# A memory-attention block between two expert layers: the second layer's hidden units in their own rows only, copied to the other rows by SBUF transfers, and a new order on GpSimd and VectorE

## The reference, cut to what matters

```python
for c0 in range(0, S, CHUNK):                      # 8 chunks of 128 tokens
    g = _grad_fn(W_state, k[:, sl], v[:, sl]) * GRAD_SCALE
    gn = jnp.maximum(jnp.linalg.norm(g, axis=-1, keepdims=True), EPS)
    g = g * jnp.minimum(MAX_GRAD_NORM / gn, 1.0)
    (S_state, W_state), Wtraj = jax.lax.scan(step, (S_state, W_state), xs)
    h = jax.nn.silu(jnp.einsum('btd,btod->bto', q[:, sl], W1t))
    outs.append(jnp.einsum('bto,btpo->btp', h, W2t))
...
out = out * jax.lax.rsqrt(jnp.mean(out * out, -1, keepdims=True) + EPS) * norm_g
```

## Time and profile before

| | |
|---|---|
| median of 3 runs (lowest, highest) | 765.0 us (764.88, 766.89) |
| span of the profiled execution | 767.1 us |
| mean granted TensorE clock in it | 0.961 |
| TensorE matmul / weight load busy | 88% / 76% |
| VectorE, ScalarE, GpSimd busy | 79%, 57%, 31% |

### The profile page before, as it was taken

The page is one execution under the profiler, slowest core; times in us unless marked ns, Lnnn a source line. Parts: engine busy times, 40 slices in busy tenths (PEclk is TensorE's granted clock), DMA queues, the critical chain, the costliest instruction groups (busy, mean ns, idle before and its releaser), DMA issues. The chain is left out here.

```text
span 767.1 us, 15489 instructions
## 1 busy us (share of the span) xinstructions
PE 673.5 (88%) x5715; PEld 580.6 (76%) x5715; DVE 606.4 (79%) x1373; ACT 438.1 (57%) x1105; POOL 240.0 (31%) x201
## 2 busy tenths in 40 slices
PE   5719999999597889999999999999998469999996
PEld 2218899898476777988879888887976257989985
DVE  0677788773488999999999999999985869887851
ACT  1325575662367667677666877767463446557550
POOL 0023453123311416052350714416061053722202
PEclk9958999999899999999999999999999769999999
DMA  9949637170411004013040311302103715834301
GB/s 343 411 176 349 221 117 254 36 214 22 126 54 56 1 1 141 27 56 112 21 146 1 105 63 56 112 1 77 35 12 100 274 49 166 281 100 163 130 15 35
DMA packets 58226, 89.26 MB, mean 116 GB/s; under 512 B 6960, under 2 KB 49072, under 8 KB 58032
## 3 DMA queue, kind: packets, MB, share of 16 engines
q1 hardware_dynamic: 46176, 70.28, 26.5%
q0 software_dynamic: 3840, 10.49, 4.2%
q10 hardware_dynamic: 8144, 7.61, 3.2%
HBM read 74.73 MB, written 22.02 MB: 126 GB/s over the span
## 5 line engine op out<-in xcount | busy, mean ns | idle before, releaser
L721 PE MATMUL ps<-moe_normedT_high,weights_high_up 128*128 128x320 f32 x252 | 80.8, 321 | 0.4 <-DVE moe_hidden_low L539 0.2
L722 PE MATMUL ps<-moe_normedT_low,weights_high_up 128*128 128x320 f32 x252 | 78.1, 310 | 0.0
L723 PE MATMUL ps<-moe_normedT_high,weights_low_up 128*128 128x320 f32 x252 | 78.1, 310 | 0.0
L1233 POOL TENSOR_TENSOR att_o_rs<-att_o_mean,minus_half 128x4 f32<-128x4 f32 x16 | 16.2, 1013 | 194.7 <-DVE att_o_mean L1491 194.7
L721 PE MATMUL ps<-weights_high_down,moe_hidden_high 128*128 128x256 f32 x256 | 73.3, 286 | 1.0 <-DVE weights_rows L547 1.0
L539 DVE SCALAR_TENSOR_TENSOR moe_hidden_low<-ps,moe_hidden_high 128x256 fp32r<-128x256 f32 x128 | 53.9, 421 | 24.3 <-ACT moe_hidden_high L676 20.2
L723 PE MATMUL ps<-weights_high_down,moe_hidden_low 128*128 128x256 f32 x256 | 71.4, 279 | 0.0
L722 PE MATMUL ps<-weights_low_down,moe_hidden_high 128*128 128x256 f32 x256 | 71.3, 279 | 0.0
L635 ACT CAST weights_high_down<-weights_raw_down 128x256 fp32r<-128x256 f32 x96 | 35.1, 407 | 38.9 <-PE ps L723 32.7
L721 PEld LDWEIGHTS ps<-weights_high_down,moe_hidden_high 128*128 128x128 f32 x256 | 48.1, 188 | 4.3 <-issue 4.3
L315 DVE TENSOR_TENSOR weights_low_down<-weights_raw_down,weights_high_down 128x256 fp32r<-128x256 f32 x128 | 49.8, 415 | 0.0
(11 more groups left out here) (328 smaller groups left out, 2073.6 us busy)
## 6 DMA issues: line engine op xcount, KB each, us to landing
weights_raw_up<-in_w SPq DMA_DIRECT2D x16, 1024.0 KB, 9.3
weights_raw_down<-in_w SPq DMA_DIRECT2D x16, 1024.0 KB, 8.3
first_xt<-in_xT SPq DMA_DIRECT2D x8, 1024.0 KB, 7.7
weights_rows<-x SPq DMA_DIRECT2D x8, 1024.0 KB, 5.6
out_x<-weights_rows SPq DMA_DIRECT2D x8, 1024.0 KB, 4.5
weights_rows<-x ACTq DMA_DIRECT2D x7, 1024.0 KB, 5.6
weights_rows<-x SPq DMA_DIRECT2D x2, 512.0 KB, 4.2
weights_raw_up<-in_w_x SPq DMA_DIRECT2D x1, 768.0 KB
```

Of the source, the lines that this page charges most:

```text
L721: mm(dst, high_l, high_r, start=start, stop=False)
L722: mm(dst, high_l, low_r, start=False, stop=False)
L723: return mm(dst, low_l, high_r, start=False, stop=stop)
L1233: g.tensor_tensor(o_rs[:, n], o_mean[:, n], t["minus_half"][:, n], ALU.pow).then_inc(o_rs_ready, 1)
```

## The change

`second_hidden` on TensorE puts the four sequences of each side only into that side's own rows: half as many products, and the result is four columns blocks wide instead of eight. ScalarE does two Silus of 64 rows x 512 columns in place of one of 128 x 1024. SyncE then copies each half to the other rows, from SBUF to SBUF, as two transfers of 64 rows x 2 KB (`double_hidden`), and `decayed_hidden` on VectorE now also waits for both of them. `second_scores` on TensorE needs own rows alone and does not wait for them.

GpSimd's `query_decay` and `mix` of the next chunk stand ahead of the first output power, and `hidden` stands between the second output power and the second residual sum of the step before. VectorE has softplus ahead of the output mean, theta ahead of the small products, and five of the eight `bn_stats` ahead of the gradients, three behind them. `last_step` has the same new order, but its hidden units are made as before, in both halves.

```diff
+            def double_hidden(c):
+                sp.wait_ge(hid2_ready, c + 1)
+                for n, own, other in SIDES:
+                    sp.dma_start(hid2[other, n, :], hid2[own, n, :]).then_inc(hid2_doubled, 16)
+            double_hidden(0)
+                if c + 2 < NCH:
+                    double_hidden(c + 1)
...
@@ -1244,18 +1254,19 @@
                 if first:
                     query_decay(c, True)
                     mix(c, True)
-                elif not last:
-                    hidden(c, par, False)
                 if norm_too:
                     norm(c + 2)
-                output_power(c, 0)
                 if not last:
                     query_decay(c + 1, False)
                     mix(c + 1, False)
+                output_power(c, 0)
+                if not last:
                     residual(c, par, 0)
                 output_power(c, 1)
                 if last:
                     return
+                if c + 2 < NCH:
+                    hidden(c + 1, 1 - par, False)
                 residual(c, par, 1)
             setup()
...
@@ -1478,6 +1501,7 @@
             def decayed_hidden(c):
                 dve.wait_ge(hid2_ready, c + 1)
+                dve.wait_ge(hid2_doubled, 32 * (c + 1))
                 v.tensor_tensor(hid2_ab[:], hid2[:], AB[:], ALU.mult).then_inc(hid2_ab_ready, 1)
             def second_scores(c, par):
...
@@ -1552,19 +1577,27 @@
             def step(c, par, first, norm_too=True):
                 split_turned(c + 1)
-                if not first:
+                if first:
+                    norm_sums(c)
+                    norm_products(c, par)
+                    softplus(c, par)
+                    thetas(c, par)
+                    gradients(c, par)
+                else:
                     slope_of(c)
+                    softplus(c, par)
                     output_mean(c - 1, 1)
                     residual(c)
-                    softplus(c, par)
                     gated_output(c - 1, 1 - par, 1)
-                gradient_norms(c, par)
-                if first:
-                    softplus(c, par)
-                elif norm_too:
-                    stats_of(c + 2)
-                thetas(c, par)
-                gradients(c, par)
+                    norm_sums(c)
+                    thetas(c, par)
+                    norm_products(c, par)
+                    if norm_too:
+                        batch_stats(c + 2, range(0, EARLY_STATS))
+                    gradients(c, par)
+                    if norm_too:
+                        batch_stats(c + 2, range(EARLY_STATS, B))
+                        aggregate(c + 2, range(B))
                 if first:
                     carry_scans(c, True)
                     decay_scans(c, True)
...
@@ -1758,7 +1791,9 @@
             def second_hidden(c):
                 act.wait_ge(pre2_made, c + 1)
-                s.activation(hid2[:], wide(DD), ACT.Silu).then_inc(hid2_ready, 1)
+                for n, own, _ in SIDES:
+                    last = s.activation(hid2[own, n, :], wide(DD)[own, 0:HALF, :], ACT.Silu)
+                last.then_inc(hid2_ready, 1)
             def retrieve(c):
                 act.wait_ge(ret_made, c + 1)
...
@@ -2034,11 +2069,13 @@
                 pe.wait_ge(qab_ready, c + 1)
                 if not first:
                     pe.wait_ge(x2_turned_copied, 2 * c)
-                for b in range(B):
-                    for rows in (slice(0, D), slice(D, P)):
-                        mm(wide(DD)[rows, b, :], state[par][:, b, D:2 * D], QAB[:, b, :], start=True, stop=False)
-                    for rows in (slice(0, D), slice(D, P)):
-                        last = mm(wide(DD)[rows, b, :], grad_w1[:, b, :], P1[:, b, :], start=False, stop=True)
+                for i in range(HALF):
+                    for n, own, _ in SIDES:
+                        b = n.start + i
+                        mm(wide(DD)[own, i, :], state[par][:, b, D:2 * D], QAB[:, b, :], start=True, stop=False)
+                    for n, own, _ in SIDES:
+                        b = n.start + i
+                        last = mm(wide(DD)[own, i, :], grad_w1[:, b, :], P1[:, b, :], start=False, stop=True)
                 last.then_inc(pre2_made, 1)
             def last_second_hidden(c, par, h):
```

More of the change, by code:

```diff
@@ L1044, in memory_attention @@
     HW = HALF * CH
+    EARLY_STATS = 5
     w_high, w_low, w_o, mean, x_norm, x_res = (
@@ L1116, in memory_attention @@
     pre2_made, hid2_ready, hid2_ab_ready = (sem(n) for n in ("pre2_made", "hid2_ready", "hid2_ab_ready"))
+    hid2_doubled = sem("hid2_doubled")
     hh_made, p2_ready, ret_made, ret_copied = (sem(n) for n in ("hh_made", "p2_ready", "ret_made", "ret_copied"))
@@ L1289, in moments_of, with batch_stats, aggregate @@
                     v.bn_stats(stats[:, b, :], x_norm[:, b, :]).then_inc(stats_done, 1)
+                aggregate(c, batches)
+            def batch_stats(c, batches):
+                if batches.start == 0:
+                    dve.wait_ge(x_loaded, 16 * c + 16)
+                    dve.wait_ge(x_normed, B * c - HALF)
+                for b in batches:
+                    v.bn_stats(stats[:, b, :], x_norm[:, b, :]).then_inc(stats_done, 1)
+            def aggregate(c, batches):
                 dve.wait_ge(stats_done, B * c + batches.stop)
@@ L1454, in residual, with norm_sums, norm_products @@
                 v.scalar_tensor_tensor(dpre[:], wide(C)[:, :, D:P], 0.5, slope[:], ALU.mult, ALU.mult).then_inc(dpre_ready, 1)
-            def gradient_norms(c, par):
+            def norm_sums(c):
                 dve.wait_ge(squared, 3 * c + 3)
                 v.tensor_reduce(nsum[:], squares[:], AX.X, ALU.add).then_inc(nsum_ready, 1)
+            def norm_products(c, par):
                 dve.wait_ge(nsum_ready, c + 1)
```

## The result

The changed kernel is slower. Its median is 778.38 us (777.24 to 781.35, four runs) against 764.94 us of the kernel before on the same chip (763.22 to 766.89, four runs): a ratio of 1.0172, 95% interval 1.0141 to 1.0204. The forecast was 767.3 us with a range of 761.5 to 772.0, so the time lies above the whole range. The profiled execution took 777.97 us at a span of 775.8.

The account below looks back on a forecast made before the run. TensorE's own work was taken to set the 46.17 us step; afterwards a loop through the transfers, 46.26 + 0.25 = 46.5 us. Seven chunks at +0.33 gave +2.3 on the 765.0 us median: 767.3 us, range 761.5 to 772.0.

Parts of the forecast that it names:

- its loop: Chain from one `decayed_hidden` to the next over VectorE, TensorE, ScalarE and the transfers: 46.26 us, 46.5 with the copies.
- the transfers' size: From the Silus' end to both transfers landed: 2.45 us taken, bounds 1.9 and 3.2; with hand-overs 2.54.
- the zero for the ends: Gains and losses in steps 0 and 6 set against each other: 0, with 2 us to either side.
- the clock: Listed only as a sign of being wrong: granted clock under 1.00 where TensorE now waits longer; no size.
- the copies' 0.25: VectorE's copies of end values, held by GpSimd's work, and what follows them: +0.25 us a step.
- TensorE -1.8 us: `second_hidden` on TensorE keeps 16 of 32 products: 1.8 us less a step.
- the Silus 1.18: ScalarE's two Silus of 64x512 in place of one of 1.03 us: 1.17 us, +0.14.
- the gradients earlier by some 3 us: VectorE's new order brings the gradients some 3 us earlier; nothing waits for that.
- the slope 0.68: VectorE's L1447, no longer held by GpSimd's first residual sum: 0.69 us instead of 1.81, -1.12.
- idle time before `decayed_hidden`: VectorE arrives there about 0.6 us before the second transfer lands and is idle, in every steady step.
- 7 x 0.33: Seven chunks have the transfers, each with a loop 0.33 us longer than 46.17: +2.3 us.
- costs all it may: Rival: transfers of 3.0 us, or copies and `mix` taking turns; steps of 47.1 to 47.4 us, 771 to 773; chance 0.19.

Follow-up runs that it names:

- ends_on_scalar: The changed kernel with the four copies of end values on ScalarE, not VectorE: 779.69 us, 1.0174 of the kernel before.
- ends_scalar_filled: ends_on_scalar with eight products on TensorE that nobody reads, ahead of `retrieve`: 770.43 us, 1.0079 of the kernel before.
- eager: The changed kernel with the first transfer started behind the first Silu, not behind both: 773.46 us, 1.0101 of the kernel before.
- filled: The changed kernel with eight 128x512 products on TensorE that nobody reads, ahead of `retrieve`: 775.33 us, 1.0125 of the kernel before.
- transfer_only: The kernel before with the second layer in own rows and the two transfers, old orders of GpSimd and VectorE: 771.28 us, 1.0076 of the kernel before.
- pool_as_before: The changed kernel with GpSimd's order of before, transfers and VectorE's order as changed: 779.78 us, 1.0181 of the kernel before.

## Why the prediction was wrong, by its own steps

The mechanism was the one it named, and its loop closes on the new trace; three terms of the sum failed: the transfers' size, the zero for the ends, and the clock, which it had left out. From `decayed_hidden` at 359.58: to `turn_keys` 16.65 us (forecast 16.54), from there to the rates 21.57 (21.28, and the copies' 0.25 on top), to the keep rates 2.01 (2.02), to the Silus' end 3.88 (3.88), to the next `decayed_hidden` 2.93 (2.54): 47.04 against 46.51.

- *Right:* TensorE -1.8 us; the Silus 1.18; the gradients earlier by some 3 us (36.56 us behind `decayed_hidden`, was 39.68), and without gain; the slope 0.68; idle time before `decayed_hidden` (1.1 us, forecast 0.6); 0.25 us for the copies, shown by ends_on_scalar and ends_scalar_filled, although all of 1.4 us is lost on VectorE.
- *Transfers, the mis-sized term.* The "2.45" from the Silus' end to both landed measured 2.84 (2.81 from the first issue), and the whole hop 2.93, not 2.54: a transfer takes 2.18 to 2.30 us, not 2.05, and the second issue comes 0.51 us behind the first, not 0.4. That is 0.39 of the 0.53 us by which the step missed its forecast. Taking the 64 KB load's 1.9 us as the base was too low; the middle of its bounds (1.9 to 3.2) was closer. eager shows that each tenth of it lengthens the step by about a tenth.
- *"0 with 2 us to either side" for the ends, wrong.* There is a loss at every chunk. Without falls (filled) `decayed_hidden` of chunk 0 comes 1.0 us later after the first gates, the five steps lose 1.0, 0.9, 0.9, 0.9 and 1.3 us, the last 1.4, because it had been short for want of statistics and now has the full loop (47.04, was 45.69), and the rest 0.4. That makes 7.8 us, where 7 x 0.33 had been forecast. The prediction had named the last one, but had set it off against gains in steps 0 and 6. In step 6 the held factor did fall from 1.86 to 0.17 us (L1495), but VectorE's wait ahead of it grew from 0.97 to 1.76 us, and the loop shows nothing of it. The first step is shorter in transfer_only (46.26 us, was 46.86), but not in filled (47.87).
- *The clock, left out of the sum.* It stood only under what would make the forecast wrong. I estimate the cost of the changed kernel's falls at 3 to 5 us: 1.0172 against 1.0125 for filled is 0.5%, with intervals that overlap, and in the profiles attention, from its first gate addition to its last `decayed_hidden` but one, is 12.1 us longer than before, and 7.8 in filled. So of these 12.1 us the prediction had 2.3; the loop and its ends have 5.5 more, the clock 4.3. The medians are 13.4 us apart; where the last 1.3 us lie, two single profiles cannot tell.

The rival "costs all it may" had the mechanism and the step (47.1 us), but multiplied by the same seven chunks without the clock it came out at 771.2. The rule held against the change, that two DMAs for two halves do not overlap (the Trainium skill, "SBUF — State Buffer", "Can I just issue two DMAs to hit both halves?"), would give about 3.0 us by the prediction's estimate; measured are 2.81, between it and my 2.45. The fixed 2.0 us in that estimate stand in a section of the Trainium skill ("DMA: Bandwidth & Descriptors", "Anatomy of one DMA") on DMAs that GpSimd issues, and these were issued from SyncE. The landings are 0.63 us apart at issues 0.51 us apart, and 0.65 at 0.62 (eager): their distance does not grow with that of the issues, which fits the rule, but no run here tests it.

It stays open why a wait of 2.1 us is followed by a fall at one chunk and not at the next, and how much of pool_as_before's long falls (10 and 7 us) was caused by its own late work.

## What to carry to other kernels

When an edit takes work off the engine that sets the step, write down where that engine will now be idle, and whether the idle time lies in one piece: here such pieces, of 2.1 us and more before a block of products, came with falls of the clock that cost an estimated 3 to 5 us beside the 7.8 us of the longer loop. The new DMA hop between two engines cost nothing that shows (1.0008) once the consumer had 3 us of other work ahead of it; look for that work first. And follow the new loop through every chunk, the first and last too, since here the chain through four engines got no shorter at the chunk where VectorE has less to do (47.04 us, was 45.69).

## What the runs showed of the hardware

- A 64x512 fp32 transfer from SBUF to SBUF (128 KB) on SyncE's queue landed 2.17 to 2.56 us after its issue in the changed kernel, but for one that took 3.48; a pair took 2.81 to 3.07 us, and once 3.99.
- Copies of 128x4 on VectorE were held by GpSimd's `tensor_tensor` to its end (1.10 and 0.60 us against 0.16); on ScalarE the same copies took 0.21 to 0.22 us while the same GpSimd instruction ran (ends_on_scalar).
- A single fall of TensorE's clock to 0.50 cost 1.7 us of its speed and made a steady step 0.7 to 1.2 us longer (47.74 and 48.23 us against 47.08 in pool_as_before); with eight unread products in the wait the clock stayed at 1.00 from 203 to 608 us (filled).
